# Experts' logits from the columns of the residual sum and of the last norm, in a two-layer graph network on one core

## What is computed

```
xn = _layernorm(x, axis=-1)
x = x + _L1_gnn_ref(xn, ...) + _L1_mix_ref(xn[None], ...)[0]                       # x2 -> x3
x = x + _L1_ffn_ref(_layernorm(x, axis=-1)[None], Wg, bg, W1, b1, W2, b2)[0]       # x3 -> out

def _L1_ffn_ref(x, Wg, bg, W1, b1, W2, b2):
    logits = x @ Wg + bg                       # 8 experts
    w, idx = jax.lax.top_k(logits, 2)
    w = jax.nn.softmax(w, axis=-1)
    h = jax.nn.silu(jnp.einsum('bsh,ehf->ebsf', x, W1) + b1[:, None, None, :])
    y = jnp.einsum('ebsf,efh->ebsh', h, W2) + b2[:, None, None, :]
    comb = jnp.einsum('bske,bsk->ebs', jax.nn.one_hot(idx, E, dtype=x.dtype), w)
    return jnp.einsum('ebsh,ebs->bsh', y, comb)
```

## Time and profile before

| | |
|---|---|
| three runs | 846.35, 1033.0, 844.45 us; median 846.35 |
| profiled execution | 843.48 us, its span 841.7 us |
| mean granted clock of TensorE | 0.974 of full |
| PE busy | 800.7 us (95%) |
| DVE, ACT, POOL busy | 539.5 (64%), 248.6 (30%), 148.2 us (18%) |

### The profile page before, as it was taken

One profiled execution on the slowest core, in us unless ns is written; L12 is line 12 of the kernel. 1 busy time (PEld: TensorE's weight loads), 2 busy tenths in 40 slices (PEclk: granted clock), 3 DMA queues, 4 the chain that ended last, 5 costly groups with the idle time before them and its releaser, 6 DMA issues.

```text
span 841.7 us, 10823 instructions
## 1 busy us (share of the span) xinstructions
PE 800.7 (95%) x3995; PEld 640.9 (76%) x3995; DVE 539.5 (64%) x743; ACT 248.6 (30%) x468; POOL 148.2 (18%) x96
## 2 busy tenths in 40 slices
PE   4999999999999999999998999997699999999997
PEld 3988766847477777765767778897598888888886
DVE  5876998979989999999777426068541111511112
ACT  4252223316411013222045332142432321432310
POOL 2011001120100000002201350031343330433300
PEclk9999999999999998999999999999589999999999
DMA  7533779796878768742041120000242120322001
GB/s 245 213 50 47 227 214 337 266 276 158 240 228 276 246 220 282 242 139 100 1 159 58 48 97 1 1 2 1 100 151 96 55 98 2 100 100 100 0 0 61
DMA packets 64211, 110.21 MB, mean 131 GB/s; under 512 B 6815, under 2 KB 16412, under 8 KB 64172
## 3 DMA queue, kind: packets, MB, share of 16 engines
q1 hardware_dynamic: 54476, 96.71, 34.5%
q0 software_dynamic: 6912, 7.70, 5.4%
q10 hardware_dynamic: 2784, 5.27, 1.7%
HBM read 105.81 MB, written 1.28 MB: 127 GB/s over the span
## 4 chain that ended last, share of the span: by engine, by line
PE 89%; DVE 6%; issue 2%; ACT 1%; POOL 1%; DVEq 0%; POOLq 0%
PE bank L1310 55%; PE bank L1730 13%; PE bank L1396 6%; PE bank L1511 4%; PE bank L1528 3%; PE bank L1522 2%; PE bank L1505 2%; PE bank L1326 1%; DVE st L890 1%; PE bank L1437 1%; PE bank L1333 1%; DVE slot L987 1%; ACT slot L581 1%; DVE slot L885 0%; DVE slot L1116 0%
## 5 line engine op out<-in xcount | busy, mean ns | idle before, releaser
L1004 DVE SCALAR_TENSOR_TENSOR weights<-weights,att 128x2048 f32<-128x2048 f32 x116 | 268.9, 2392 | 2.7 <-DMA weights<-in_L_gnn_basis 2.1
L1291 DVE CAST hid_hi<-slot 128x626 fp32r<-128x626 f32 x32 | 15.6, 487 | 160.7 <-ACT slot L846 160.7
L1310 PE MATMUL bank<-half,ew_hi 128*128 128x314 f32 (+1 forms) x512 | 114.0, 312 | 2.2 <-POOL ew_lo L550 2.2
L1310 PE MATMUL bank<-AT,slot 125*128 125x312 f32 (+1 forms) x400 | 105.9, 426 | 0.8 <-ACT slot L711 0.8
L1310 PEld LDWEIGHTS bank<-AT,slot 125*128 125x128 f32 x400 | 75.5, 189 | 31.0 <-ACT slot L711 1.0
L550 POOL TENSOR_TENSOR ew_lo<-weights,ew_hi 128x1024 fp32r<-128x1024 f32 x28 | 69.4, 2500 | 134.4 <-ACT ew_hi L828 134.4
L1310 PEld LDWEIGHTS bank<-half,ew_hi 128*128 128x128 f32 x512 | 88.4, 193 | 5.6 <-issue 2.9
L581 ACT ACTIVATE slot<-bank 128x312 f32<-128x312 f32 (+6 forms) x88 | 43.8, 525 | 148.7 <-PE bank L1310 128.9
L1310 PE MATMUL bank<-weights,slot 128*125 128x512 f32 (+5 forms) x306 | 86.9, 447 | 0.3 <-ACT slot L581 0.3
L846 ACT ACTIVATE slot<-bank,eb_now 128x312 f32<-128x312 f32 x64 | 33.3, 522 | 157.2 <-PE bank L1310 157.2
L1310 PE MATMUL bank<-half,ew_lo 128*128 128x312 f32 (+1 forms) x256 | 79.5, 310 | 0.0
(11 more groups left out here) (297 smaller groups left out, 1116.4 us busy)
## 6 DMA issues: line engine op xcount, KB each, us to landing
weights<-in_L_gnn_basis SPq DMA_DIRECT2D x60, 1024.0 KB, 5.5
weights<-in_L_ffn_W SPq DMA_DIRECT2D x32, 512.0 KB, 4.5
weights<-in_L_mix_kqv_w SPq DMA_DIRECT2D x1, 3072.0 KB, 10.2
weights<-in_w_qkvT SPq DMA_DIRECT2D x3, 1024.0 KB, 5.4
slot<-slot POOLq DMA_DIRECT2D x10, 250.0 KB, 6.5
weights<-in_L_mix_mlp_w ACTq DMA_DIRECT2D x2, 1024.0 KB, 13.6
weights<-in_L_gnn_root ACTq DMA_DIRECT2D x2, 1024.0 KB, 8.7
slot<-in_row_mlp_b POOLq DMA_DIRECT2D x1, 1250.0 KB, 26.1
```

The source lines that it names most:

```text
L1004: ins = dve.scalar_tensor_tensor(wrel[layer][r], wmat(at), att[:, layer, r, b:b + 1], wrel[layer][r], ALU.mult, ALU.add)
L1310: ins = pe.matmul(out, a, b, start=i == 0, stop=i == len(pairs) - 1)
```

## The change

The logits no longer wait for the normalised rows. With Wg' = Wg less its column mean over the features (wgc), the logits of a normalised row are (x3 @ Wg') / std + bg; all are multiplied by std here, so raw logits x3 @ Wg' + bg * std are compared. x3 is x2 plus res, so x3 @ Wg' = (xn2 @ Wg') * std of x2 + res @ Wg', where xn2 (the norm that opened the layer) still lies in columns in col(2), and res lies in columns too. A ninth column of wgc, 1/512, gives the mean of res. Then:
- PE: 4 matmuls for the column sums of Wg (wgs) behind ha; the logits' 20 matmuls of col(2) and 8 of res ahead of the first two sum rows, 12 more of res ahead of the last three; en ahead of the transposes of the normalised rows.
- DVE: no statistics, no normalising; a few small operations instead; the list before the one-hots as before. xe_low moves from POOL to DVE, from the bank, behind comb.
- ACT: a square with a sum for each row tile, one root for all, five normalised rows behind x3_rs, five copies to xe_hi; the copies to col(2) are gone.
- bmv and bsd keep the batch norms' statistics apart, so that mv and sd still hold those of x2.

The diff, cut to its core:

```diff
-              ("kv", 3), ("qfT", 4), ("xk", 5), ("at", 2), ("xv", 5), ("atT", 1), ("xkv", 1), ("ha", 1),
-              ("xq", 8), ("xo", 8), ("xpr", 13),
-              ("xeT", 5), ("el", 1), ("en", 1), ("combT", 2), ("eb2", 5), ("eh", 3)]
+              ("kv", 3), ("qfT", 4), ("xk", 5), ("at", 2), ("xv", 5), ("atT", 1), ("xkv", 1), ("ha", 1), ("wgs", 1),
+              ("xq", 8), ("xo", 8), ("xpr", 15),
+              ("en", 1), ("xeT", 5), ("combT", 2), ("eb2", 5), ("eh", 3)]
...
-XP_TILE, X3_TILE = (0, 1, 2, 3, 4, 6, 8, 9), (5, 7, 10, 11, 12)
+XP_TILE, EL_TILE, X3_TILE = (0, 1, 2, 3, 4, 5, 9, 10), (6, 11), (7, 8, 12, 13, 14)
...
+            pool.wait_ge(S("psum_full"), filled("xpr", 15))
             pool.memset(comb72.bitcast(f32), 0.0).then_inc(S("pads"), 1)
-            for j in range(TT):
-                pool.wait_ge(S("xe_col"), j + 1)
-                pool.wait_ge(S("act_read"), READ0["xeT"] + j + 1)
-                pool.tensor_tensor(xe_lo[:, :, P * j:P * j + P], col(2)[:, :, P * j:P * j + P],
-                                   xe_hi[:, :, P * j:P * j + P].bitcast(f32), ALU.subtract).then_inc(S("xe_low"), 1)
-
             pool.wait_ge(S("elist"), 2)
...
-            for j in range(TT + 1):
-                if j < TT:
-                    sqrt_of_tile("xe_row", 0, j)
-                if j:
...
-                    act.activation(col(2)[:, :, P * j - P:P * j], tile, ACT.Copy).then_inc(S("xe_col"), 1)
-                    copy_out("xeT", j - 1, xe_hi[:, :, P * j - P:P * j], tile)
+            for j in range(TT):
+                act.wait_ge(S("x3r_out"), j + 1)
+                act.wait_ge(S("less_mean"), 1 if j < 2 else 2)
+                ins = act.activation(row(1)[:, j, :], x[:, j, :], ACT.Square, bias=less_mean[:, j:j + 1], accum_out=var3[:, j:j + 1])
+            link(ins)
+            act.activation(std3, var3, ACT.Sqrt, bias=eps[0:P, 0:1], scale=1.0 / H).then_inc(S("x3_std"), 1)
+            act.wait_ge(S("x3_rs"), 1)
+            for j in range(TT):
+                act.activation(row(1)[:, j, :], x[:, j, :], ACT.Identity, scale=rs3[:, j:j + 1], bias=shift3[:, j:j + 1]).then_inc(S("xe_row"), 1)
+            for j in range(TT):
+                copy_out("xeT", j, xe_hi[:, :, P * j:P * j + P], B("xeT", j)[:, 0:KT * P].rearrange("p (k t) -> p k t", k=KT))
             act.wait_ge(S("gap"), 3)
             act.activation(eexp, eexp, ACT.Exp).then_inc(S("gap_exp"), 1)
...
+            dve.memset(wgc[:, :, E1:E1 + 1], 1.0 / H)
+            dve.wait_ge(S("psum_full"), filled("wgs", 1))
+            dve.wait_ge(S("Wg_in"), 32)
+            dve.scalar_tensor_tensor(wgc[:, :, 0:E1], B("wgs")[:, 0:E1].unsqueeze(1).to_broadcast([128, KT, E1]), -1.0 / H, Wg,
+                                     ALU.mult, ALU.add).then_inc(S("wgs_out"), 1)
...
             def x3_row(j):
-                for n in ((0, 1, 2, 3, 4), (5,), (6, 7), (), ())[j]:
-                    xp_tile(n)
                 dve.wait_ge(S("psum_full"), filled("xpr", X3_TILE[j] + 1))
                 dve.tensor_tensor(x[:, j, :], B("xpr", X3_TILE[j])[0:P, :], x[:, j, :], ALU.add).then_inc(S("x3r_out"), 1)
-                dve.wait_ge(S("x3r_out"), j + 1)
-
-            layernorm_by_tile(x, row(1), "xe_row", x3_row)
             U = [table(6, i, E1) for i in range(6)]
-            dve.wait_ge(S("psum_full"), filled("el", 1))
-            dve.wait_ge(S("Wg_in"), 32)
-            dve.tensor_tensor(U[0], B("el")[0:P, 0:TT * E1].rearrange("p (j e) -> p j e", j=TT),
-                              small[0:P, 0:E1].unsqueeze(1).to_broadcast([P, TT, E1]), ALU.add).then_inc(S("el_out"), 1)
-            dve.wait_ge(S("el_out"), 1)
+            mean2 = mv[0:P, :, 0:1].rearrange("p j o -> p (j o)")
+
+            def raw_logits(i, j0, j1):
+                res_part = B("xpr", EL_TILE[i])[0:P, (E1 + 1) * j0:(E1 + 1) * j1].rearrange("p (j e) -> p j e", e=E1 + 1)
+                dve.scalar_tensor_tensor(less_mean[:, j0:j1], res_part[:, :, E1:E1 + 1].rearrange("p j o -> p (j o)"), -1.0, mean2[:, j0:j1],
+                                         ALU.mult, ALU.subtract).then_inc(S("less_mean"), 1)
+                dve.tensor_tensor(U[0][:, j0:j1, :], res_part[:, :, 0:E1], U[4][:, j0:j1, :], ALU.add).then_inc(S("el_out"), 1)
+
+            for n in range(6):
+                xp_tile(n)
+            dve.wait_ge(S("psum_full"), filled("xpr", EL_TILE[0] + 1))
+            link(dve.tensor_tensor(U[4], B("xpr", EL_TILE[0])[0:P, 64:64 + TT * E1].rearrange("p (j e) -> p j e", e=E1),
+                                   bc(sd[0:P, :], E1), ALU.mult))
+            raw_logits(0, 0, 2)
+            x3_row(0)
+            x3_row(1)
+            xp_tile(6)
+            xp_tile(7)
+            dve.wait_ge(S("psum_full"), filled("xpr", EL_TILE[1] + 1))
+            raw_logits(1, 2, TT)
+            for j in range(2, TT):
+                x3_row(j)
+            dve.wait_ge(S("x3_std"), 1)
+            dve.wait_ge(S("el_out"), 2)
+            link(dve.tensor_tensor(U[1], small[0:P, 0:E1].unsqueeze(1).to_broadcast([P, TT, E1]), bc(std3, E1), ALU.mult))
+            link(dve.tensor_tensor(U[0], U[0], U[1], ALU.add))
             largest(U[0])
...
-            dve.tensor_tensor(eexp, top2, top1, ALU.subtract).then_inc(S("gap"), 1)
+            link(dve.reciprocal(rs3, std3))
+            dve.tensor_tensor(shift3, less_mean, rs3, ALU.mult).then_inc(S("x3_rs"), 1)
+            link(dve.tensor_tensor(eexp, top2, top1, ALU.subtract))
+            dve.tensor_tensor(eexp, eexp, rs3, ALU.mult).then_inc(S("gap"), 1)
...
+            for j in range(TT):
+                dve.wait_ge(S("act_read"), READ0["xeT"] + j + 1)
+                dve.tensor_tensor(xe_lo[:, :, P * j:P * j + P], B("xeT", j)[:, 0:KT * P].rearrange("p (k t) -> p k t", k=KT),
+                                  xe_hi[:, :, P * j:P * j + P].bitcast(f32), ALU.subtract).then_inc(S("xe_low"), 1)
             for j in range(TT):
...
             ins.then_inc(S("psum_full"), 1)
+            bk = claim(pe, "wgs")
+            pe.wait_ge(S("Wg_in"), 32)
+            group(bk[:, 0:E1], [(ones[:, :], Wg[:, k, :]) for k in range(KT)]).then_inc(S("psum_full"), 1)
...
-            for n in range(8):
+            def res_logits(bk, j):
+                return group(bk[0:P, (E1 + 1) * j:(E1 + 1) * (j + 1)], [(res[:, k, P * j:P * j + P], wgc[:, k, :]) for k in range(KT)])
+
+            for n in range(6):
                 projected(n)
-                if n in (4, 5):
-                    sum_row(n - 4)
+            bk = claim(pe, "xpr", EL_TILE[0])
+            pe.wait_ge(S("wgs_out"), 1)
+            for j in range(TT):
+                group(bk[0:P, 64 + E1 * j:64 + E1 * j + E1], [(col(2)[:, k, P * j:P * j + P], wgc[:, k, 0:E1]) for k in range(KT)])
+            pe.wait_ge(S("xp_out"), 4)
+            res_logits(bk, 0)
+            res_logits(bk, 1).then_inc(S("psum_full"), 1)
+            for j in range(2):
+                sum_row(j)
+            projected(6)
+            projected(7)
+            bk = claim(pe, "xpr", EL_TILE[1])
+            pe.wait_ge(S("xp_out"), 8)
+            for j in range(2, TT):
+                ins = res_logits(bk, j)
+            ins.then_inc(S("psum_full"), 1)
             for j in range(2, TT):
                 sum_row(j)
-
-            def expert_logits(j):
-                pe.wait_ge(S("xe_col"), j + 1)
-                return group(B("el")[0:P, E1 * j:E1 * j + E1], [(col(2)[:, k, P * j:P * j + P], Wg[:, k, :]) for k in range(KT)])
-
-            pe.wait_ge(S("Wg_in"), 32)
-            for j in range(TT):
-                tile_to_cols("xeT", j, j, row(1), "xe_row")
-                if j == 1:
-                    claim(pe, "el")
-                if j:
-                    expert_logits(j - 1)
-            expert_logits(TT - 1).then_inc(S("psum_full"), 1)
             bk = claim(pe, "en")
             pe.wait_ge(S("selected"), 1)
             group(bk[0:1, 0:E1], [(ones[0:P, 0:1], table(6, 5, E1).rearrange("p j e -> p (j e)")[:, 0:E1])]).then_inc(S("psum_full"), 1)
+            for j in range(TT):
+                tile_to_cols("xeT", j, j, row(1), "xe_row")
             pe.wait_ge(S("comb"), 1)
             for n in range(2):
                 bk = claim(pe, "combT", n)
```

24 lines of the change are left out of this document (15 added, 9 removed).

## The result

The changed kernel takes **852.24 us** (median of six, 845.19 to 854.84) against 845.58 for the kernel before in the same comparison: ratio **1.0085, interval 1.0061 to 1.0109**. The forecast was 842.2 with a range up to 846.5. It is outside the range, and on the other side of no change: 7 us slower.

A forecast was written before the change was run, and what follows sets the result against it. PE is busy 95% of the span; what counts is when the experts' first matmul starts. Comb 2.6 us earlier gives 840.9 for the profiled execution, 842.2 from the three runs' mean of 844.8; range 838.6 to 846.5.

The forecast's parts named there:

- Four matmuls for the column sums of Wg: On PE before xq, where PE has no gap: 0.106 us each, +0.4 us on everything behind.
- The projections: On PE behind the sixth projection: 28 narrow matmuls, 3.0 us; the eighth projection ends at 584.7 instead of 583.3, +1.4.
- The sum's rows: PE does 12 narrow matmuls (1.3 us) ahead of the last 12 transposes (1.55); DVE ends row 4 at about 589.0.
- the first rival: Clock falls in PE's narrow block ahead of the last projections: 3.4 us fall costs 1.7, time 843.9; chance 0.20.
- The slower rival: Clock falls inside the narrow block and stays at half for 6.9 us: costs 3.45, time 845.6; chance 0.08.
- the 44 narrow ones all cost 0.21: Bound on PE's narrow matmuls: the chain grows by 4.6 us and the kernel is 2.0 slower; 0.106 was taken.
- Squares on ACT: ACT's squares of the sum's rows start 0.70 us apart; row 4 ends at 590.05, the root at 590.35.
- The decision: DVE from logits to count of choices takes 1.4 us, until 591.8; list's last cast at 594.3 instead of 601.18.
- What stands on ACT behind the list: Rows, copies, table load, exponential until 599.8, end unmoved; comb 2.6 us earlier, the experts' first matmul at 608.2 instead of 610.8.
- the longer load: Rival: ACT's table load holds the exponential beyond its 1.28 us; 1.0 us lost, time 843.2; chance 0.03.
- xe_low on DVE: Five subtractions on DVE behind comb, 601.6 to 604.9; eb2 and x4 follow before 608.2, so no wait.
- PE without a gap before the sum's first rows: Sign expected in the profile after: PE shows no idle gap ahead of the sum's first rows.

The follow-up runs named there:

- the spread version: The changed kernel with its twenty matmuls of the last norm's columns placed four behind each of the first five projections; 845.24 us, ratio 1.0036 to the kernel before.

## Why the prediction was wrong

*Four matmuls for the column sums of Wg*: forecast +0.4; they are 8 passes, 0.85. Mis-sized.

*The projections*: **this is the step that failed.** "Behind it come 20 + 8 narrow matmuls, 28 x 0.106 = 3.0 us" multiplies a price per record by a count from the code. The row that gave the price could have shown it: the earlier trace rows has x8 for one row of the logits, for which the code writes four. In place of 3.0 the block took 5.94 at the full clock (+3.0), and 9.40 with the fall in it (+3.5). The projections behind it, two at 4.22 instead of 3.5, and eight transposes at 2.05 instead of 0.9, add 0.7 and 1.1. *The sum's rows*: 12 matmuls for 1.3 were 24 passes in 2.76 (+1.5). With the 0.4 above, these make 10.2; to the end of row 4 the miss is 10.4, in the whole stretch 10.1.

Of this, 4.7 is the count (0.4 + 3.0 + 1.3). It turns the gain of 2.6 into a loss of 2.1 at the same clock, and the spread version shows such a loss: 3.0 by the ratio, 2.65 in its stretch. Most of the rest is the first rival, **the clock falls in the narrow block**, to which I gave 0.20. Its condition came true more strongly than it was written, since the block was twice as long as I had it, 5.9 us against the 4.4 of the stages that it was compared with. The comparison had the same mistake in it: the "40 matmuls" of the gates are 40 records too, of 20 matmuls in the code. In records it was 40 against 56, not 40 against 28, and the "against" (it is shorter) falls away. The slower rival (the fall lasts) has the right mechanism too: 10.2 us at half, against the 6.9 it had. No case combined the fall with a wrong count, so none reached 847.

The stated bound, "the 44 narrow ones all cost 0.21", doubles the price for the clock's sake and comes to 4.6, the count's miss by luck. As a bound it failed: 88 passes at 0.21 are 18.5 us, 14 above the 4.7 that the forecast had for them.

*Squares on ACT*: rows 0.73 and 0.77 apart, expected 0.70; the root ends 1.18 after the sum's row 4, expected 1.35. *The decision*: the count ends 1.43 after the root, expected 1.45, and the list's last cast 2.0 after the count, 2.5 expected. The claim that the list comes **7 us earlier** is false: measured from kvb it comes 2.9 later. *What stands on ACT behind the list*: 3.64, 2.45, 1.28, 0.21, comb 1.84 after the exponential, then 1.05 and 2.36. Each is within 0.3 of its forecast. But the exponential was to stand unmoved at 599.6; in that clock it ended at 609.9. Here the chance of the longer load can be judged: the operation starts 1.30 after the load's start. The Trainium skill (ScalarE: Activation LUTs, What ACT_TABLE_LOAD costs) puts the load at about 1.28 us, and the row agrees; the drain of 1.38 that it adds doesn't show, neither ahead of the load, which starts as the last copy ends (611.57), nor behind it: the exponential begins 0.02 after the end of its load. *xe_low on DVE* ended at 617.85, before the loop's start, and nothing waited for it. The loop kept its two passes.

"PE without a gap before the sum's first rows" came out right, and it is the mistake seen from the other side: what is put there is paid in full. Before, 40 passes made the logits, the first eight between PE's waits for DVE's norm, the other 32 without a gap. The change replaces them by 88, all ahead of the last sum rows: 8 for the column sums, 40 for the last norm's part and 40 for the sum's part. The forecast saw 44.

## What to carry to other kernels

Take count and price from the same row. If a row's count isn't the code's, the instruction is more than one pass, and fp32 operands are two here (not in transposes). Small matmuls are only free in a stage where PE waits; read the idle time ahead of each before counting. Here 56 narrow passes in one piece brought the clock down for 10 us, with the critical work behind them; the same passes in portions between wide matmuls did not, in the executions that were profiled.
